# All 128 rows for the relation table's third part and for lent edges in a two-layer graph attention kernel

## The reference

```python
rel = rel_w[edge_relations]                      # 64 relations
mod_k = K[src] + 0.2 * rel[:, None, :]
scores = jnp.einsum('ehd,ehd->eh', Q[dst], mod_k) / D ** 0.5
...                                              # softmax over the edges of one destination
agg = jax.ops.segment_sum(w[:, :, None] * V[src], dst, num_segments=N)
...
out = msgs.reshape(N, H * D) @ Wo + bo
```

## Time and profile before

| What | Value |
|---|---|
| Median of three runs | 4631.05 us (4630.45 to 4632.06) |
| The profiled execution's span | 4627.2 us |
| First attention, from 375 to 2460 us | 2085 us: PE busy 1982.2, DVE 1621.5, POOL 1492.6, ACT 1137.0 |
| Granted TensorE clock there | 1.00 |
| From 2460 us to the end (second attention) | 2167 us: PE busy 1645.5, granted clock 0.76 |
| PE, DVE, POOL, ACT over the whole span | 85%, 74%, 68%, 60% |

### The profile page before, as it was taken

The page is one execution under the profiler, slowest core; times in us unless marked ns, Lnnn a source line. Parts: engine busy times, 40 slices in busy tenths (PEclk is TensorE's granted clock), DMA queues, the critical chain, the costliest instruction groups (busy, mean ns, idle before and its releaser), DMA issues. The chain is left out here.

```text
span 4627.2 us, 149696 instructions
## 1 busy us (share of the span) xinstructions
PE 3929.3 (85%) x42462; PEld 2568.6 (56%) x42462; DVE 3415.2 (74%) x11602; ACT 2795.2 (60%) x7985; POOL 3143.2 (68%) x3229
## 2 busy tenths in 40 slices
PE   6988999999999999999996778778877877777874
PEld 4655555555555555555554556555555555555553
DVE  3235788777777778777775578888778778787777
ACT  2324555555555555555553677777777777777775
POOL 1217777777777777777772777777777777777773
PEclk9998999999999999999997677777778777787777
DMA  6878888888888888888884777777777777777774
GB/s 207 282 236 246 259 259 259 257 259 259 259 255 260 258 260 258 257 258 261 259 256 120 187 206 206 207 204 205 207 207 205 205 204 205 205 208 209 203 206 131
DMA packets 820558, 1052.06 MB, mean 227 GB/s; under 512 B 458633, under 2 KB 632338, under 8 KB 820464
## 3 DMA queue, kind: packets, MB, share of 16 engines
q0 software_dynamic: 225072, 726.83, 53.9%
q1 hardware_dynamic: 594078, 323.35, 27.0%
q10 hardware_dynamic: 1314, 0.99, 0.1%
HBM read 915.79 MB, written 133.39 MB: 227 GB/s over the span
## 5 line engine op out<-in xcount | busy, mean ns | idle before, releaser
L1286 POOL DMA_INDIRECT plain_rows<-xp,plain_index x1563 | 1559.8, 998 | 554.9 <-issue 440.8
L765 POOL DMA_INDIRECT typed_rows<-kv,typed_index x1563 | 1511.2, 967 | 626.2 <-issue 414.3
L1391 PE MATMUL plain_p_o<-plain_rows,plain_weight_t 128*64 128x130 f32 (+1 forms) x8336 | 856.5, 348 | 44.0 <-DVE plain_weight_t L1417 43.3
L1158 ACT ACTIVATE typed_weight<-typed_weight,typed_col 128x416 f32<-128x416 f32 x521 | 334.6, 642 | 855.0 <-DVE typed_col L991 809.5
L1378 PE MATMUL plain_p_s<-all_cst,plain_rows 128*128 128x128 f32 (+1 forms) x2084 | 455.0, 318 | 368.2 <-DMA plain_rows<-xp,plain_index 365.9
L1391 PEld LDWEIGHTS plain_p_o<-plain_rows,plain_weight_t 128*64 128x64 f32 (+1 forms) x8336 | 570.2, 169 | 203.8 <-issue 128.5
L1378 PEld LDWEIGHTS plain_p_s<-all_cst,plain_rows 128*128 128x128 f32 (+1 forms) x2084 | 335.2, 174 | 522.6 <-issue 504.8
L989 DVE CUSTOM_DVE_ANT_0 typed_weight<-typed_p_s,typed_far 128x416 f32<-128x416 f32 x521 | 305.1, 586 | 371.5 <-PE typed_p_s L874 347.8
L874 PE MATMUL typed_p_s<-typed_kt,typed_q 64*32 64x416 f32 x4168 | 472.4, 521 | 103.4 <-issue 73.0
L1424 DVE CUSTOM_DVE_ANT_0 plain_alpha<-plain_alpha,plain_far 128x416 f32<-128x416 f32 x521 | 310.0, 595 | 311.4 <-ACT plain_alpha L1540 296.4
L962 DVE TENSOR_TENSOR typed_kt<-typed_p_kt,typed_rel 128x768 f32<-128x768 f32 x521 | 494.7, 950 | 3.7 <-PE typed_p_kt L851 3.4
(11 more groups left out here) (190 smaller groups left out, 6303.5 us busy)
## 6 DMA issues: line engine op xcount, KB each, us to landing
typed_match<-match SPq DMA_DIRECT2D x131, 208.0 KB
plain_match<-match SPq DMA_DIRECT2D x131, 208.0 KB
agg<-qkv_zero SPq DMA_DIRECT2D x98, 264.0 KB
typed_agg<-agg SPq DMA_DIRECT2D x98, 264.0 KB
plain_agg<-agg SPq DMA_DIRECT2D x98, 264.0 KB
kv<-qkv_kv SPq DMA_DIRECT2D x98, 258.0 KB
typed_kinds<-match SPq DMA_DIRECT2D x131, 192.0 KB
typed_rows<-kv,typed_index POOLq DMA_INDIRECT x1563
```

The lines of the kernel that those rows point to most:

```text
L765: pool.indirect_dma_start(rows[:, r, j, :], None, k.kv, bass.IndirectOffsetOnAxis(ap=index[:, g, at:at + 1], axis=0)).then_inc(rows_in[r], 16)
L1158: act.activation(weight[:, c], weight[:, c], ACT.Exp, bias=col[:, t.slot(4), LOW:LOW + 1]).then_inc(exp_done, 1)
L1286: pool.indirect_dma_start(rows[:, r, j, :], None, k.xp, bass.IndirectOffsetOnAxis(ap=index[:, g, at:at + 1], axis=0)).then_inc(rows_in[r], 16)
L1391: last = pe.matmul(p_o[at:at + HC, t.slot(2), 0:2 * V], weight_t[0:e, t.slot(2), j * P + at:j * P + at + HC], val[:, 2 * V * g:2 * V * g + ...
```

## The change

Two matmuls of the first attention take all 128 rows. In `relate`, L843 contracts over all of `rel_b` and all of `hit`; for that, the setup on DVE fills rows 0 to 63 of `rel_b` with the third part of the table and sets rows 64 to 127 to zero (a copy of 128 rows becomes a copy of 64 and a memset of 64). In `aggregate`, the lent edges' chunk contracts over all 128 rows of `weight_t`, whose rows 32 to 127 are zero there, with the first 128 rows of the next tile's values.

```diff
-                pe.matmul(p_r[:, 0:MAIN], rel_b[0:REL], hit[0:REL, t.slot(2)], start=False, stop=True).then_inc(related, 1)
+                pe.matmul(p_r[:, 0:MAIN], rel_b[:], hit[:, t.slot(2)], start=False, stop=True).then_inc(related, 1)
...
                 for j in range(CH + 1):
-                    e = P if j < CH else SPILL
-                    v = rows[0:e, t.slot(R), j] if j < CH else rows[0:e, t.back(-1).slot(R), 0]
+                    v = rows[:, t.slot(R), j] if j < CH else rows[:, t.back(-1).slot(R), 0]
                     for h in range(HEADS):
                         at = TN * h
-                        last = pe.matmul(p_o[at:at + TN, 0:V], weight_t[0:e, t.slot(2), j * P + at:j * P + at + TN], v[:, D + V * h:D + V * h + V],
+                        last = pe.matmul(p_o[at:at + TN, 0:V], weight_t[:, t.slot(2), j * P + at:j * P + at + TN], v[:, D + V * h:D + V * h + V],
                                          start=j == 0, stop=j == CH, tile_position=(0, at), skip_group_check=True)
...
-            init(v.tensor_copy(rel_b[:], rel_w[:, 2]))
+            init(v.tensor_copy(rel_b[0:REL], rel_w[0:REL, 2]))
+            init(v.memset(rel_b[REL:P], 0.0))
```

## The result

The changed kernel takes 4584.4 us (median of four runs, 4582.9 to 4586.0) against 4631.6; the ratio is 0.9901, interval 0.9889 to 0.9913. The forecast was 4586. The profiled span fell from 4627.2 to 4581.9 us.

The account below looks back on a forecast made before the run. PE was taken to bound the first attention only around its 96 updates, DVE or the scores/add_keys ring elsewhere. Updates 37.4 us plus hand-over 7.7 make 45 us: 4631 - 45 = 4586 us, range 4550 to 4618.

Parts of the forecast that it names:

- What bounds the kernel: First attention: PE sets the pace behind each of 96 updates; in other tiles DVE or the scores/add_keys ring does.
- A stage bound by PE throughout: Rival, first attention: PE bounds every tile, 201 us would go but POOL binds after 178, 4453 us; chance 0.10 for 4453–4575.
- Relate, 0.25 to 0.26 us a tile: Relate and the transposes behind it: 0.10 us saved twice at changes of rows, 0.05 on the first transpose pair.
- Aggregate, 0.13 us: Lent edges' last two sets of four matmuls in aggregate: 0.23 us falls to 0.11, taken as 0.13 saved per tile.
- Updates, 37.4 us: PE's path from scores to scores over an update: 0.39 us saved at each of 96 updates, 37.4 us.
- the hand-over, 7.7 us: DVE's add_keys after a wait for scores: 0.06 us less waiting for the arrival, four times per 16 tiles, 7.7 us.
- The loads that wait on: Rival, relate and aggregate: weight loads still wait with equal rows, nothing saved, 4631 us; no change had chance 0.07.
- POOL: POOL's gathers in the first attention: room for 45 us, its wait for free slots shorter by some 45 us.
- The clock: Rival, first attention: longer PE waits lower the granted clock from 1.00; 0.92 eats the gain, 0.76 gives 4751 us; chance 0.05.

Follow-up runs that it names:

- around the updates: Changed kernel with wide rows only in the relate and aggregate steps around updates, 4 of 16 tiles each, 64 and 32 rows elsewhere: 4595.5 us, ratio 0.9923.
- elsewhere: Changed kernel with wide rows only in the other 12 of 16 tiles, 64 and 32 rows in the steps around updates: 4618.6 us, ratio 0.9976.

## Why the prediction was right

*What bounds the kernel.* Right: DVE's waits for the scores and PE's waits ahead of them were the evidence, and the pair of kernels around the updates and elsewhere shows it directly: 35.1 us from a quarter of the tiles, 9.0 us from the rest. A stage bound by PE throughout, 201 us, is out.

*Relate, 0.25 to 0.26 us a tile.* Right: L842 to L900 took 0.27 + 0.26 + 0.71 = 1.24 us and takes 1203.25 - 1202.26 = 0.99.

*Aggregate, 0.13 us.* Right: 0.79 to 0.66 us. Together 5.84 to 5.48 over this update, 0.36, against 0.39 of the forecast.

*Updates, 37.4 us, and the hand-over, 7.7 us.* Right in kind, and two small errors cancel. An update gained 0.36 us, 96 x 0.36 = 34.6, and around the updates 35.1 us were measured. The hand-over gained more than 7.7: of DVE's 183 waits that end with the scores, add_keys came over 1.10 us behind L989 (L988 after) in 181 before and in 15 after, and its distance from L989, summed over the 519 tiles that show it, fell by 10.0 us. With wide rows elsewhere it fell by 6.8 of the 9.0 us, around the updates by 0.5.

*The loads that wait on, as the rule of the Trainium skill has it* ("TensorE: Matmul & The Clock Gate", section "Part 3: Packing small matmuls — row/col tiling"). Out. The load of L843 starts at 1202.27, 0.01 us behind that of L842 and while its matmul runs, with the same rows. In relate the load waited 0.17 us where its rows differed from those ahead, and doesn't where they are the same. Equal rows alone don't always free a load, though: the aggregate's first load, 128 rows behind the 128 of L860, still sits idle for 0.2 us (below).

*POOL.* A miss without effect: its wait for free slots was to fall by the 45 us, from 178.3, and fell by 70, to 108.7, while its issue time rose from 408.8 to 438.9.

*The clock.* It stayed at 1.00 in the first attention although PE's waits grew, so the forecast's only slow case didn't come.

## What to carry to other kernels

A matmul with fewer rows than those around it cost PE time twice here, 0.10 us at each change of rows and up to 0.10 more for the first float32 pair behind it; where its operands can be padded with zero rows at no cost, pad them. What that brings is not the saved time by the number of tiles: an engine that is busy for 95% can still wait for another in most tiles (327 of 521 here), and only the stretches in which the other engine waits for it shorten the program. Find these in the list of waits, price the edit there, and move work out of them when the padding is done.

## What the runs showed of the hardware

The granted clock of the second attention, a mean over its two levels of 1.2 and 2.4 GHz, was 0.76 where one matmul in six there (those over lent edges) took 32 rows, 0.79 with 64 and 0.83 with 128, at the same stage length and the same number of matmuls. In the run with 64 rows the changes of rows were all left, so, if its value holds, it isn't their absence alone; but it rests on one run close to the spread of the others. It brought no time there, since gathers set that stage's pace, and why the clock differed stays open.

The cost of a change of rows depended on what followed: 0.05 us more behind it for single transposes, 0.10 for the two-pass float32 matmuls of an update.

Not every such wait comes from the rows. In the kernel after, from 375 to 2415 us, the aggregate's loads still wait:

```profile
PEld typed_p_o L888 <- issue: 89.0, 421, 0.2
```

It was 89.2 us, 422 times, before. Its first matmul starts 0.20 us after L860, 1199.47 to 1199.67, where each transpose of L859 is followed by the next start after 0.11 us; both sides have 128 rows. The work changes there from transposes to pieces at 32-column positions; no run here tells whether that is the cause.
